# The input load of each window of the last feed-forward stage, with one of its waits left out

## The reference

```python
x = x + 0.5 * ffn(layernorm(x), w1, conv_w, conv_b, w2)
x = x + attn(layernorm(x), slope, qkvu_w, qkvu_b, out_w, out_b, theta)
x = x + 0.5 * ffn(layernorm(x), w1, conv_w, conv_b, w2)

def ffn(x, w1, conv_w, conv_b, w2):
    h = bit_linear(x, w1)                    # 1024 -> 4096
    h = depthwise_conv1d(h, conv_w, conv_b)  # 3 taps along the sequence
    return bit_linear(silu(h), w2)           # 4096 -> 1024

def bit_linear(x, w):  # rows of x rounded to 8 bits, w to -1, 0, 1 times a scale
    return act_quant(x) @ weight_quant(w).T
```

## Time and profile before

| | |
|---|---|
| median of 12 runs | 8420.39 us (8411.96 to 8431.83) |
| the profiled execution | 8425.03 us |
| its span on the slowest core (core 5) | 8423.5 us |
| spans of the other cores | 8363.5 to 8412.3 us |
| PE, DVE, ACT, POOL busy | 45%, 45%, 14%, 9% |
| mean granted TensorE clock | 0.720 of full |
| second feed-forward stage | from 5996 us to the end |

### The profile page before, as it was taken

One profiled execution on the slowest core, in us unless ns is written; L12 is line 12 of the kernel. 1 busy time (PEld: TensorE's weight loads), 2 busy tenths in 40 slices (PEclk: granted clock), 3 DMA queues, 4 the chain that ended last, 5 costly groups with the idle time before them and its releaser, 6 DMA issues.

```text
span 8423.5 us, 53790 instructions; the slowest of 8 cores (8363.5 to 8423.5 us)
## 1 busy us (share of the span) xinstructions
PE 3828.0 (45%) x15718; PEld 1576.9 (19%) x15718; DVE 3828.8 (45%) x6552; ACT 1209.0 (14%) x1870; POOL 797.3 (9%) x747
## 2 busy tenths in 40 slices
PE   0035454554555543555555553333344455344454
PEld 0011111111111111222222221111111121111122
DVE  4345655544565562222222223444346455345554
ACT  0011211202112120111111111101112111111210
POOL 0002102020220211000000000000022022022012
PEclk9977776766777766776777776655677777677676
DMA  3422231233222215000000001111232233332234
GB/s 121 146 73 77 68 85 60 70 88 83 90 70 70 75 57 138 6 6 6 5 6 4 4 3 55 40 50 50 70 100 70 85 90 90 100 100 75 70 100 105
DMA packets 576699, 560.48 MB, mean 67 GB/s; under 512 B 368898, under 2 KB 508482, under 8 KB 555810
## 3 DMA queue, kind: packets, MB, share of 16 engines
q1 hardware_dynamic: 521138, 454.28, 18.2%
q0 software_dynamic: 55280, 102.77, 4.5%
HBM read 475.23 MB, written 92.27 MB: 67 GB/s over the span
## 4 chain that ended last, share of the span: by engine, by line
PE 36%; DVE 32%; DMA 13%; ACT 9%; issue 7%; another core or an unknown queue 1%; POOL 1%; DVEq 1%; ACTq 0%; POOLq 0%; SPq 0%
DVE Rh L587 4%; PE psD L397 4%; PE psA L1036 3%; DVE ar L517 3%; DVE g L540 3%; PE psA L762 3%; PE psB L1036 3%; ACT g L560 3%; PE psB L762 3%; PE psG L762 2%; PE psE L762 2%; DMA wba<-wq2s 2%; PE psF L762 2%; DMA wbb<-wq2g 2%; PE psA L885 2%
## 5 line engine op out<-in xcount | busy, mean ns | idle before, releaser
L574 POOL TENSOR_TENSOR g<-g,hbc 128x512 f32<-128x512 f32 (+2 forms) x640 | 711.8, 1142 | 2889.9 <-DVE hbc L345 2869.5
L587 DVE TENSOR_SCALAR Rh<-g 128x512 bf16<-128x512 f32 (+2 forms) x640 | 652.0, 1079 | 116.6 <-POOL g L574 103.9
L788 DVE TENSOR_REDUCE bca<-g 128x512 f32<-128x2048 f32 (+1 forms) x112 | 409.5, 3656 | 282.0 <-ACT g L560 282.0
L560 ACT ACTIVATE g<-g 128x512 f32<-128x512 f32 (+1 forms) x512 | 279.8, 616 | 849.3 <-DVE hedge L553 849.1
L1036 PE MATMUL psA<-y,wqh 128*128 128x512 bf16 x1024 | 277.1, 419 | 212.1 <-ACT cosf L987 79.2
L762 PE MATMUL psA<-rp,wba 128*128 128x512 bf16 x384 | 156.1, 580 | 347.8 <-DMA wba<-wq1s 182.0
L1069 DVE COPY vtm<-psT 128x512 bf16<-128x512 bf16 x64 | 27.2, 424 | 626.0 <-PE psT L1064 619.7
L1036 PE MATMUL psB<-y,wqh 128*128 128x512 bf16 x1024 | 255.1, 394 | 95.1 <-ACT silk L1048 31.8
L354 PE MATMUL psF<-identf,bca 128*128 128x128 f32 (+1 forms) x132 | 36.3, 426 | 426.3 <-DVE bca L792 245.7
L762 PE MATMUL psA<-rp,wbb 128*128 128x512 bf16 x512 | 152.4, 451 | 165.1 <-ACT g L560 165.1
L885 PE MATMUL psA<-Rh,wba 128*128 128x512 bf16 (+1 forms) x512 | 146.1, 456 | 159.3 <-DMA wba<-wq2s 145.9
(11 more groups left out here) (323 smaller groups left out, 7809.7 us busy)
## 6 DMA issues: line engine op xcount, KB each, us to landing
wba<-wq1s SPq DMA_DIRECT2D x64, 1024.0 KB
wbb<-wq1s SPq DMA_DIRECT2D x64, 1024.0 KB
wba<-wq2g SPq DMA_DIRECT2D x64, 1024.0 KB
wbb<-wq2g SPq DMA_DIRECT2D x64, 1024.0 KB
wba<-wq2s SPq DMA_DIRECT2D x48, 1024.0 KB
wbb<-wq2s SPq DMA_DIRECT2D x32, 1024.0 KB
xs<-ar POOLq DMA_DIRECT2D x14, 2048.0 KB, 13.9
wfull<-w1T SPq DMA_DIRECT2D x1, 16384.0 KB
```

The lines of the kernel that those rows point to most:

```text
L560: vsil = k.rec("sc", lambda e, c=c, ncol=ncol: e.activation(g[:, c * 512:c * 512 + ncol], g[:, c * 512:c * 512 + ncol], AF.Silu), wait=[(" ...
L574: vpool = k.rec("gp", lambda e, hc=hc, w=w: e.tensor_tensor(g[:, hc * 512:hc * 512 + w], g[:, hc * 512:hc * 512 + w], hbc[:, 0:w], ALU.mul ...
L587: vR = k.rec("ve", lambda e, hc=hc, w=w: e.tensor_scalar(Rh[:, hc * 512:hc * 512 + w], g[:, hc * 512:hc * 512 + w], MAGIC, -MAGIC, ALU.add ...
L788: k.rec("ve", lambda e, gslc=gslc, w=w: e.reduce_max(bca[:, 1024:1024 + w], gslc, AX.X, apply_absolute_value=True), wait=[("sc", k.v("sc") ...
```

## The change

In `ffn` the value of the counter of GpSimd's transfers is now taken once, when the stage begins (`rq_gd`). The load of `rp` waits for that value in place of the counter's value at the call, and no longer waits for VectorE. Its waits for the last matmul that reads `rp` (`w1te`) and for the SP load before it stay. In the first feed-forward stage `rq_src` is None, and this branch is not taken.

```diff
@@ -694,6 +694,7 @@
             wins.append((sqi, 2, None, 1))
         NW = len(wins)
+        rq_gd = k.v("gd")
         wb_free = {id(wba): 0, id(wbb): 0}
@@ -731,8 +732,7 @@
                 v_rpq[wi] = ("ld", k.dma(
                     "sy", rp[:].rearrange("p (c t) -> p c t", c=NCH),
                     _drv(rq_src)[:, :, sqi * S + t0:sqi * S + t0 + TT],
-                    wait=[("te", st8["w1te"]), ("ve", k.v("ve")),
-                          ("gd", k.v("gd"))]))
+                    wait=[("te", st8["w1te"]), ("gd", rq_gd)]))
```

## The result

| | before | changed |
|---|---|---|
| median of the runs | 8420.02 us | 8317.27 us |
| lowest to highest | 8411.96 to 8439.53 | 8310.88 to 8327.69 |
| span of the profiled execution, slowest core | 8423.5 us (core 5) | 8317.9 us (core 7) |
| second feed-forward stage, mean of the cores | 2426.4 us | 2318.7 us |

The ratio of the runs is 0.9878, with a 95% interval from 0.9869 to 0.9887: 1.2% faster, 103 us by the medians. The last line is worked out from each core's span and the moment of the stage's first load (`xa<-xs`). It is the better measure of this change, since the stages before it differ by some tens of microseconds between cores and executions: 107.7 us came out of the stage.

What follows compares the result with a forecast made beforehand. Hand-overs bound the kernel: SP's load of `rp` waits needlessly for VectorE's sums. Gains of 95.9 + 16.0 = 111.9 us from 8425.0 give 8313.1, less 4.6 for the median, 8308 us; range 8288 to 8330.

Steps and rivals of the forecast that it cites:

- The shift of SP's chain in the six windows: Windows 0, 1, 2, 5, 6, 7: load of `rp` goes out when the last `wq2g` load lands; gain 95.9 us.
- Window 4: Kind 2: load of `rp` follows the landing of `xb` instead of the copy to `hbc`; gain 16.04 us.
- The rule of the Trainium skill that was weighed there: Window 4: queues share 16 DMA engines; beside window 3's store, `rp` takes up to twice 6.65 us, whole sum 105 us.
- Everything behind moves along: After `fc` 5 in the six windows: later loads, last sums, store, `xload` and next window shift along with it.
- How long the moved loads take: `rp` plus `wq2s`: 11.1 to 15.3 us, middle taken; 13 us either way in six windows, 3 more in window 4.
- The rival with more traffic: Seven windows: each of two moved loads takes some 4.5 us longer, giving back 63 us; 8371 us, chance 0.05.
- the one that ends slower than before: Seven windows: `rp` and `wq2s` each take 11 us longer beside other cores' 2 MB transfers; 8463 us, chance 0.02.
- The clock holds: `fc` 5 in six windows: shorter pause keeps 2.4 GHz, 1.7 to 2.9 us back in each; 8294 us, chance 0.05.
- It does nothing: Load of `rp`: the real releaser may be another counter that stays; 8420 us, chance 0.03.
- the pause before `fc` 5: TensorE before `fc` 5 in psA: pause becomes about 10 us, still ending with the load of `wq2s`.

Runs made afterwards that it cites:

- the kernel of the first section that keeps the wait for VectorE: Against the kernel before, only the counter of GpSimd's transfers is taken once at the stage's beginning; 8428.3 us, ratio 1.0001.
- the first experiment: Halves of the change against the kernel before: without the wait for VectorE 8331.6 us, ratio 0.9881; with the transfer counter taken once alone 8428.3 us, 1.0001.
- the two traces above: The changed kernel, 8317.27 us; and the changed kernel with the wait for VectorE put back in the windows of kind 0 and 1, 8410.3 us.

## Why the prediction was right

The mean of the cores, before and changed, in pieces: from ScalarE's first convolution instruction of a window to GpSimd's issue of its store (windows 0, 1, 2, 5, 6, 7), from window 3's store to window 4's, and from a store to ScalarE's start in the next window.

| piece | before | changed | gain | forecast |
|---|---|---|---|---|
| window 0 | 255.7 | 241.9 | 13.8 | 14.7 |
| window 1 | 270.3 | 252.0 | 18.3 | 16.7 |
| window 2 | 268.9 | 251.8 | 17.1 | 16.5 |
| window 5 | 254.4 | 239.5 | 14.9 | 15.0 |
| window 6 | 268.5 | 253.4 | 15.1 | 16.5 |
| window 7 | 268.1 | 251.9 | 16.2 | 16.5 |
| sum of the six | | | 95.4 | 95.9 |
| window 4 | 95.4 | 81.1 | 14.3 | 16.0 |
| seven starts after a store, sum | 150.1 | 153.8 | -3.7 | 0 |

The forecast was 8308 us and the median is 8317, inside the range of 8288 to 8330.

*The shift of SP's chain in the six windows* was right in place and size. VectorE's sums had held the load, the load goes out at the landing before it, and the load of `wq2s` still leads TensorE. That the sum came within 0.5 us is partly luck: the terms were read on one core, the single windows miss by up to 1.6 us, and the misses cancel.

*Window 4* gave 1.7 us less. The term rests on when the load of `xb` lands: 17.08 us after its issue in the earlier trace rows, on the mean of the cores `rp` now follows after 18.5. On the slowest core of the changed kernel (chain of waits):

```profile
7087.84 18.04 DMA xb<-xs
...
7105.95 5.42 DMA rp<-rq
...
7111.44 10.17 DMA wba<-wq2s
```

The rule of the Trainium skill that was weighed there ("DMA: Bandwidth & Descriptors", section "Issuing engines are not separate DMA queues") shows in the load of `xb`, beside the store, but hardly in that of `rp` behind it, which took 5.42 us here, and 6.3 us from issue to issue on the mean, 5.9 before. The prediction says that no row times that store; the trace does. Before, it was issued at 7141.71 and landed 18.7 us later, 2 us behind the load of `xb`. In the changed kernel it is still on its way when `rp` goes out, but only for another 2.0 us as the mean of the cores (0.7 to 4.2). So the condition of the rule was met, and what it could cost was small. The first load of `wq2s` behind it took 10.17 us on this core, but the mean of the cores rose only from 6.2 to 6.8.

*Everything behind moves along* held but for 3.7 us, which the starts after a store lost together, half a microsecond each on the mean. Not all of it need come from the change: the kernel of the first section that keeps the wait for VectorE, as slow as before, has 151.6 there against 150.1. Windows 3, 8 and 9, which load no `rp`, kept their length, as the prediction asked: 246.8, 246.9 and 63.7 us became 247.2, 246.8 and 62.6.

*How long the moved loads take* was the open term. From issue to issue, `rp` takes 5.9 us in the six windows (5.7 before) and `wq2s` 6.2 (6.0 before), near the middle that was taken. The rival with more traffic would have needed 4.5 us more for each, the one that ends slower than before 11.

*The clock holds* was wrong, as forecast: with pauses of 3.8 to 8.6 us psA's 32 matmuls still take 8.49 to 9.83 us where psB's take 7.07. Behind the pause of 7.50 us in window 1 the granted clock was 0.50 from 6518 to 6521 us, the lower level. *It does nothing* fell with the first experiment.

What I had too long is the pause before `fc` 5: about 10 us, from window 1's slow pair of loads, where the six windows of the slowest core show 3.8 to 8.6. It hid how near VectorE's residual sum stood: the prediction has it end 7 us ahead of the load, and with the load of `rp` ahead it became the limit after a gain of 3.0 us a window.

Of the 111.9 us forecast the pieces hold 106.0, the stage 107.7 and the medians 103. The pieces leave out windows 3, 8 and 9 and the stage's first loads.

## What to carry to other kernels

A counter that stands for "all of an engine's work so far" is a safe wait and can be a needless one. Where transfers go one at a time through a queue, a needless wait at one of them delays all behind it, as here, so look for the queue's longest pause with nothing in flight, and ask what of the program order the load at its end needs. The gain is the issue time less the landing of the load before it, and whether it lasts is read from what the consumer waits for next: here the next limit stood 3 us inside the loads' landing, and the same look at the window's end gave another 65 us by the medians.

## What was not expected of the hardware

A load of 2 MB (`xb`) beside this core's store of 2 MB took 17.08 us in the earlier trace rows, 18.04 and 19.9 in the two traces above, where the same load had taken 8.54 us at the start of the stage in the trace of the kernel before (issued at 6004.90), with nothing else of the core's on the way. The kernel with the load of x late bears it out: as the mean of the cores, the loads that it moves away from the store take 8.8 to 9.4 us from issue to issue, where those at the ends of windows 0, 1, 5 and 6 took 15.1 to 18.4 in the changed kernel.

The eight cores run the same program some tens of microseconds apart, and a load of 1 MB in the same place of the changed kernel takes from 5.0 to 7.8 us (`rp`) and from 5.5 to 10.2 (`wq2s`) from issue to issue, depending on the core and the window.
